# Attention over 31 pipelined steps: V's product in four visits, division on GpSimd, V's own copy of X

## The reference, cut to what matters

```
x1 = x + sum_h softmax(mask(q_h k_h^T / 8)) v_h W_o,h + b_o     (q, k, v from the layer-normed x)
out = x1 + FFN(layernorm(x1))                                   (sigmoids, router, 8 experts, top 2)
```

## Time and profile before

| | us |
|---|---|
| median of 3 runs (1163.03 to 1163.51) | 1163.17 |
| the profiled execution | 1161.71 |
| its span | 1160.0 |
| TensorE busy | 1039.1 (90%) |
| VectorE busy | 903.1 (78%) |
| ScalarE busy | 703.5 (61%) |
| GpSimd busy | 658.7 (57%) |

### The profile page before, as it was taken

How to read it: one execution, slowest core, us unless ns; L and a number is a source line. 1 busy time by engine, 2 the same in 40 slices (tenths; PEclk the granted TensorE clock), 3 DMA queues, 4 the chain that set the end, 5 groups by cost and what they waited for, 6 DMA issues and landing times.

```text
span 1160.0 us, 51334 instructions
## 1 busy us (share of the span) xinstructions
PE 1039.1 (90%) x19852; PEld 772.4 (67%) x19852; DVE 903.1 (78%) x2180; ACT 703.5 (61%) x1474; POOL 658.7 (57%) x658
## 2 busy tenths in 40 slices
PE   5689999999999999999999999999999848699984
PEld 3577777777777777777777777777777636354542
DVE  6878888888888888888888888888888863547573
ACT  4656666666666666666666666666666542577664
POOL 5766666666656666666666666665666202244644
PEclk9999999999999999999999999999999877899998
DMA  7677777777777776777777777777777740132422
GB/s 172 164 182 172 174 169 173 169 173 172 171 167 181 165 175 168 168 168 168 168 170 174 175 172 170 171 169 172 173 173 170 179 91 21 38 84 47 91 50 60
DMA packets 127279, 173.06 MB, mean 149 GB/s; under 512 B 46096, under 2 KB 57360, under 8 KB 127248
## 3 DMA queue, kind: packets, MB, share of 16 engines
q1 hardware_dynamic: 127248, 172.67, 64.3%
HBM read 117.67 MB, written 21.36 MB: 120 GB/s over the span
## 4 chain that ended last, share of the span: by engine, by line
PE 71%; DVE 13%; DMA 5%; issue 5%; ACT 3%; SPq 2%; POOL 1%; DVEq 0%; POOLq 0%; ACTq 0%
PE ZB L658 25%; PE SPS L641 12%; PE SPS L642 10%; PE ZB L626 8%; DVE PTZ L918 4%; PE ZB L631 4%; DMA XTB<-xt_scratch 4%; PE ZB L666 3%; DVE SSB L975 2%; SPq L416 2%; PE SPS L817 1%; PE SPS L791 1%; PE ZB L832 1%; PE ZB L826 1%; PE ZB L809 1%
## 5 line engine op out<-in xcount | busy, mean ns | idle before, releaser
L975 DVE CUSTOM_DVE_ANT_0 SSB<-SPS,MASK 128x640 f32<-128x640 f32 (+7 forms) x512 | 372.0, 745 | 124.6 <-PE SPS L642 111.1
L641 PE MATMUL SPS<-KHP,QS 128*128 (+2 forms) x768 | 326.2, 430 | 33.5 <-DVE NM L975 28.7
L658 PE MATMUL ZB<-PTZ,VR 32*64 32x256 f32 (+2 forms) x16384 | 322.7, 295 | 21.4 <-DVE PTZ L918 19.0
L1278 ACT ACTIVATE PRL<-SSB,NM 128x640 f32<-128x640 f32 (+3 forms) x256 | 253.3, 989 | 144.9 <-DVE NM L975 144.4
L658 PEld LDWEIGHTS ZB<-PTZ,VR 32*64 32x64 f32 x16384 | 271.5, 131 | 69.3 <-issue 53.9
L483 POOL TENSOR_TENSOR X<-X,OT 128x512 f32 (+1 forms) x64 | 81.9, 1279 | 342.3 <-ACT OT L1288 333.9
L642 PE MATMUL SPS<-KLP,QS 128*128 (+2 forms) x768 | 261.4, 348 | 0.0
L918 DVE STREAM_TRANSPOSE PTZ<-PRL 128x640 f32<-128x640 f32 (+3 forms) x256 | 258.6, 1030 | 0.0
L1278 ACT ACTIVATE PRS<-SSB,NM 128x128 f32<-128x128 f32 (+3 forms) x256 | 142.5, 559 | 154.4 <-DVE NM L975 154.4
L641 PEld LDWEIGHTS SPS<-KHP,QS 128*128 128x128 f32 x768 | 145.3, 189 | 110.9 <-issue 47.2
L466 POOL TENSOR_TENSOR QS<-RAW,QS 64x512 fp32r<-64x512 f32 x128 | 165.3, 1292 | 10.3
(11 more groups left out here) (167 smaller groups left out, 999.6 us busy)
## 6 DMA issues: line engine op xcount, KB each, us to landing
VR<-v_scratch SPq DMA_DIRECT2D x256, 256.0 KB, 5.6
KHP<-KHP SPq DMA_DIRECT2D x64, 256.0 KB, 3.2
KLP<-KLP SPq DMA_DIRECT2D x64, 256.0 KB, 3.9
v_scratch<-V SPq DMA_DIRECT2D x32, 512.0 KB, 7.7
RSB<-rcp_scratch SPq DMA_DIRECT2D x64, 256.0 KB, 4.0
XTB<-xt_scratch SPq DMA_DIRECT2D x62, 256.0 KB, 3.4
VR<-gate_scratch SPq DMA_DIRECT2D x16, 512.0 KB, 5.9
WQK<-in_W_q SPq DMA_DIRECT2D x33, 64.0 KB, 3.2
```

Of the source, the lines that this page charges most:

```text
L641: pe.matmul(SP_[n % 2][:, c0:c0 + wc], q, kh[:, c0:c0 + wc], start=True, stop=False)
L658: last = pe.matmul(ZB[h * DH:(h + 1) * DH, i, kt * TR:QT * TR], VR[rows, j, kt, h * DH:(h + 1) * DH], turned_block(h, kt, j, rows), start= ...
L975: v.tensor_tensor_reduce(out=SSB[n % 2][:, 0:w], in0=SP_[n % 2][:, 0:w], in1=MASK[:, S - w:S], scale=1.0, scalar=BIG, op0=ALU.add, op1=ALU ...
L1278: act.activation(exps_of(n), SSB[n % 2][:, 0:w], ACT.Exp, bias=NM[:, col:col + 1], scale=-1.0, accum_out=L[:, col:col + 1]).then_inc(exp_d ...
```

## The change

- **TensorE.** Units 5 and 6 are computed ahead of the product with V, whose blocks are now visited as 0 and 1; 2 and 3; 4 and 5; 6 and 7. At the step's end the order is unit 13, V, units 14 and 15, output projection (before: units 13 and 14, V, output projection, unit 15).
- **Division.** ScalarE copies the undivided product from ZB to the place in PTZ where the divided one stood (`act_z`, two copies), ahead of exponential 12. GpSimd divides there, in place (`divide`, two instructions of 128x512), ahead of its first `add_out`. VectorE's four instructions go. V's product waits for the first copy only.
- **ScalarE.** Exponential 15 moves from behind piece 0 of the next body to between the two output copies, which both move behind exponential 14.
- **VectorE.** Turn 13 moves ahead of mask 0, masks 5 and 6 ahead of turns 0 and 1, turns 2 and 3 behind masks 7 and 8, turn 8 ahead of mask 11, mask 15 ahead of turn 12.
- **V's X.** V reads a second copy of X transposed, XW, loaded once per step in one DMA of 512 KB (`stage_xv`). XTB is reloaded as soon as the four pieces of Q and K have read it. `spread_sums` waits in addition until GpSimd is past the last division, since that reads RSB.

```diff
         def stage_x(sp, it, c):
-            sp.wait_ge(v_filled, it * 2 + c - 1)
+            if isinstance(it, int) and it == 2:
+                sp.wait_ge(v_filled, 3 + c)
+            else:
+                sp.wait_ge(qk_filled, it * 4)
+                sp.nop(nofuse=True)
+            sp.dma_start(XTB[:, c * CH:(c + 1) * CH], xt_dram[:, part]).then_inc(x_staged[c], DMA)
+
+        def stage_xv(sp, it):
+            sp.wait_ge(v_filled, it * 2)
             sp.nop(nofuse=True)
-            sp.dma_start(XTB[:, c * CH:(c + 1) * CH], xt_dram[:, part]).then_inc(x_staged[c], DMA)
+            sp.dma_start(XW[:, :], xt_dram[:, bass.ds(((it // HP) % B) * S, S)]).then_inc(xv_staged, DMA)
...
+        def divide(gp, it, g):
+            gp.wait_ge(z_copied, it * 2 + 2)
+            gp.wait_ge(r_spread, it * (2 * DMA) + 2 * DMA)
+            gp.nop(nofuse=True)
+            z = ZN[g].rearrange("p (t i r) -> p i t r", i=P // TR, r=TR)
+            gp.tensor_tensor(z, z, RSB[:, g, :].rearrange("p (i t r) -> p i t r", t=TC, r=TR), ALU.mult).then_inc(zn_done, 1)
...
                 if not first:
+                    divide(gp, it - 1, 0)
+                    divide(gp, it - 1, 1)
                     add_out(gp, it - 1, 0)
...
-            values(0, 1)
             scores(5, 6)
...
-            values(2)
+            values(0, 1)
             scores(7, 8)
...
-            values(3)
+            values(2, 3)
...
-            scores(13, 14)
+            scores(13)
             v_of(0)
             v_of(1)
+            scores(14, 15)
             out_of(0)
             out_of(1)
-            scores(15)
...
+            turn_back(13)
             mask(0)
...
-            turn_back(13)
             turn_back(14)
...
-            turn(6, 7)
+            turn(6, 7, 8)
             stats(5)
             mask(11)
-            turn(8)
             mask(12)
...
-            for k in range(4):
-                zn(k)
             turn(9)
...
+            mask(15)
             turn(12)
-            mask(15)
...
+        def act_z(act, it, k):
+            banks = slice(2 - k * 2, 4 - k * 2)
+            act.wait_ge(pv_done, it * QT + QT)
+            act.activation(PTZ[:, QT * 9 * P:QT * 9 * P + 2 * CH].rearrange("p (q i r) -> p i q r", i=P // TR, r=TR)[:, banks],
+                           ZB[:, banks, 0:QT * TR].rearrange("p i (q r) -> p i q r", r=TR), ACT.Copy).then_inc(z_copied, 1)
...
-            exps_to(11, 13)
+            exps_to(11, 12)
+            if not first:
+                act_z(act, it - 1, 0)
+                act_z(act, it - 1, 1)
+            exps_to(12, 13)
             v_of(0)
...
             v_of(1)
-            out_of(0)
...
             exps_to(14, 15)
+            out_of(0)
+            exps_to(15, 16)
             out_of(1)
```

More of the change, by code:

```diff
@@ L214, in build_program @@
         x_staged = [sem(f"x_staged{c}") for c in range(2)]
+        xv_staged = sem("xv_staged")
         keys_spread = [sem(f"keys_spread{c}") for c in range(2)]
@@ L222, in build_program @@
         v_early = sem("v_early"); v_late = sem("v_late")
-        pv_done = sem("pv_done"); zn_done = sem("zn_done")
+        pv_done = sem("pv_done"); z_copied = sem("z_copied"); zn_done = sem("zn_done")
         bias_filled = sem("bias_filled"); bias_ready = sem("bias_ready")
@@ L331, in spread_sums @@
             sp.wait_ge(r_written, it * (2 * DMA) + 2 * DMA)
+            if isinstance(it, int) and it == STEPS - 1:
+                sp.wait_ge(zn_done, it * 2)
+            else:
+                sp.wait_ge(q_split, it * 4 + 8)
             for h in range(2):
@@ L368, in body @@
                 else:
+                    if not last:
+                        stage_xv(sp, it + 1)
                     spread_sums(sp, it - 1)
@@ L378, in body @@
                     spread(sp, it + 1, 1 - par, 1)
+                    if not first:
+                        stage_x(sp, it + 2, 0)
+                        stage_x(sp, it + 2, 1)
                 spread_v(sp, it, half, par, 0)
-                if not last:
+                if first:
                     stage_x(sp, it + 2, 0)
@@ L574, in _ @@
             norm_in(1, 1)
+            divide(gp, STEPS - 1, 0)
+            divide(gp, STEPS - 1, 1)
             add_out(gp, STEPS - 1, 0)
@@ L628, in pe_v @@
         def pe_v(pe, it, s, bank):
+            xt = XTB if isinstance(it, int) and it < 2 else XW
             for k in range(TC):
                 t = s * TC + k
-                last = pe.matmul(bank[:, k * P:(k + 1) * P], XTB[:, t * P:(t + 1) * P],
+                last = pe.matmul(bank[:, k * P:(k + 1) * P], xt[:, t * P:(t + 1) * P],
                                  WV[:, bass.ds((it % HP) * 2, 2), :].rearrange("p h e -> p (h e)"), start=True, stop=True)
@@ L663, in pe_out @@
         def pe_out(pe, it, g, bank):
-            pe.wait_ge(zn_done, it * 4 + 4)
+            pe.wait_ge(zn_done, it * 2 + g + 1)
             for i in range(TC):
@@ L710, in v_of @@
                 else:
-                    pe.wait_ge(zn_done, it * 4 - 2)
+                    pe.wait_ge(z_copied, it * 2 - 1)
+                    if s == 0:
+                        pe.wait_ge(xv_staged, it * DMA)
                 pe_v(pe, it + 1, s, ZB[:, 2 + s, :])
@@ L1036, in back @@
                     dve_reciprocal(v, it - 1, 1 - par)
-            def zn(k):
-                if not first:
-                    dve_zn(v, it - 1, k)
+            turn_back(13)
             mask(0)
@@ L1060, in dve_step @@
             stats(1)
-            if first:
-                mask(5)
+            mask(5)
+            mask(6)
             turn(0, 1)
-            if not first:
-                mask(5)
-            mask(6)
             stats(2)
-            turn(2, 3)
             stats(3)
@@ L1071, in dve_step @@
             mask(8)
+            turn(2, 3)
             turn(4, 5)
@@ L1210, in _ @@
             dve_low(v, 0, 0)
-            for k in range(4):
-                dve_zn(v, it, k)
             gates_1(v, 0)
@@ L1319, in act_step @@
                 qk(0)
-                act_exp(act, it - 1, 1 - par, UNITS - 1)
                 exps_to(0, 1)
@@ L1350, in act_step @@
             exps_to(14, 15)
+            out_of(0)
+            exps_to(15, 16)
             out_of(1)
-            if last:
-                act_exp(act, it, par, UNITS - 1)
         @block.scalar
@@ L1431, in _ @@
             turn_of(1)
+            act_z(act, STEPS - 1, 0)
+            act_z(act, STEPS - 1, 1)
             act_out(act, STEPS - 1, 0, Z)
```

8 lines of the change are left out of this document (removed).

## The result

| | us |
|---|---|
| before, median of 4 runs (1163.03 to 1171.34) | 1163.34 |
| after, median of 4 runs (1234.02 to 1240.31) | 1236.16 |
| ratio, with its 95% interval | 1.0622 (1.0588 to 1.0655) |
| profiled execution of after, span 1238.6 | 1240.31 |

The change makes the kernel 6.2% slower. The prediction had the direction and a place for it, but 1210 us, with a range up to 1224: the loss is 73 us where 47 were forecast. The profiled execution is the slowest of the four, 4 us above their median; sums over its trace explain 1240.31, not 1236.16.

A forecast was written before the change was run, and what follows sets the result against it. The prediction took the kernel as bound by TensorE with a thin cover at the seam of two bodies. 1161.71 profiled + 46.4 (29 steps) + 2.7 (tail) - 1.4 (body 31) = 1209.4, plus 1.5 to the median: 1210; range 1166 to 1224.

The forecast's parts named there:

- Points 4 and 5: At the seam: GpSimd's add starts at 514.28 (before 513.12); piece 2 waits for the second output copy, 516.28 instead of 515.39.
- Point 6: VectorE: turn 15 ends at 520.15, masks 3 and 4 behind it, so the 0.62 us wait becomes longer, on masks.
- Point 7: GpSimd's splits of Q end at 519.75, holding piece 3's bias copy and exponential 1; mask 3 starts at 521.08, not 520.63.
- Point 8: Behind mask 3, units 5 and 6: the product with V starts at 522.70 instead of 519.90, 2.80 us later.
- Point 9: Unit 9 starts at 530.33, 1.79 us later; a step takes 30.0 us against 28.40 on average, +46.4 us over 29.
- signs of being wrong: Prediction wrong if product with V starts within 6.5 us of piece 0, or piece 2 follows piece 1 without gap.
- The unseen costs: GpSimd's divisions 0 to +1.1 us per step, taken as 0; XW's reload nothing; behind the last step +2.7, body 31 -1.4.
- The port lock: GpSimd and VectorE share ports exclusively; could delay GpSimd's add some 1.2 us per step, 35 us in all; left out.
- the sum: Whole kernel: 1161.71 + 46.4 + 2.7 - 1.4 = 1209.4 us; median 1.5 above, 1210.9, stated as 1210.
- The open circle: Seam rival: second copy in time, piece 3 not waiting for the splits; step 28.56 us, 1169 us in all; chance 13%.
- The division as a gate: Rival: GpSimd's division over 2 us each makes the output's second half wait, 0.5 us per step, 1225 us; chance 3%.
- The faster case: Rival: VectorE's lead reaches mask 4, no seam stop; saves 0.62, 0.20, 0.6; step 26.8, 1118 us (half: 1140); chance 16%.

The follow-up runs named there:

- e5: The changed kernel with ScalarE's first output copy ahead of exponential 14 again and five filler matmuls between units 4 and 5: 1200.95 us, ratio 1.0336.
- e3: The changed kernel with five filler matmuls of 512 columns between units 4 and 5, their result overwritten: 1213.63 us, ratio 1.0448.
- e1: The changed kernel with ScalarE's first output copy put back ahead of exponential 14: 1232.9 us, ratio 1.0595.
- e10: The changed kernel with the filler matmuls, piece 2 waiting for the first output copy only and piece 3 for the second: 1238.59 us, ratio 1.0623.
- e4: The kernel before with V's own copy of X alone (XW, XTB reloaded early): 1157.97 us, ratio 0.9956.
- e7: V's own copy and GpSimd's division, with a new order of the loop's bodies meant to leave no engine waiting at the seam: 1116.78 us, ratio 0.9599.
- e8: The kernel before with own copy, GpSimd's division and units 5 and 6 ahead of the product in four visits: 1205.35 us, ratio 1.0363.
- e6: The kernel before with V's own copy and GpSimd's division with ScalarE's two copies, otherwise the old order: 1146.84 us, ratio 0.9852.
- e9: e8 with five filler matmuls between units 4 and 5, their result overwritten: 1171.9 us, ratio 1.0055.

## Why the prediction was right in direction and too small

It was right about the order and wrong about the clock. The starts that its points give, beside those on the trace of after, whose piece 0 starts at 526.81. In the trace of before, piece 0 starts at 513.26 in the same view, and the schedule starts it where the old body did, so the forecasts stand 13.55 us later here. The line of before, in that view:

```profile
513.26 1.02 PE L626 MATMUL ZB<-XTB,WQK 128*128 128x512 f32 x2
```

| point | forecast + 13.55 | measured |
|---|---|---|
| 4, GpSimd's add starts | 527.83 | 527.69 |
| 5, piece 2 starts | 529.83 | 529.71 |
| 6, turn 15 starts | 532.54 | 532.69 |
| 7, splits of Q end | 533.30 | 533.15 |
| 7, mask 3 starts | 534.63 | 534.52 |
| 8, product with V starts | 536.25 | 536.29 |
| 9, unit 9 starts | 543.88 | 543.67 |

**Points 4 and 5** hold within 0.14 us. The first output copy behind exponential 14 delays GpSimd's add; e5 against e3 gives that move a price of 0.5 us per step, and e1's full-clock steps 0.44.

**Point 6** is where the prediction chose, and it held: the wait for turns went (19.0 us to none), and the waits for masks grew (28.7 to 77.1). Turn 15 was 0.15 us later than laid out; it cost nothing, because point 7 comes later still.

**Point 7** was laid out as the link that decides. The chain goes through it, and e10 takes the other link away without a gain: without the wait before piece 2 the full-clock step is the same. That point 5's wait appears in the profile with 21.8 us says nothing of its price.

**Point 8.** From piece 0 to the product the order of time has 9.48 us now and had 6.64 before (513.26 to 519.90; the chain of the earlier trace rows dates piece 0 at 513.43), so +2.84 against +2.80.

**Point 9** and the step: 29.96 against 30.0. Unit 9 came 0.2 us sooner than laid out, so the agreement of the step to 0.04 is in part luck. Of the signs of being wrong neither came: the product with V starts 9.48 us behind piece 0, and piece 2 has its gap. Ahead of unit 5 about 2 us of idle time were forecast and 1.56 came. The second wait that was forecast, ahead of unit 6, is not among the idle times: unit 6 follows unit 5 at 535.62.

**The unseen costs.** The division took 1.29 us where 1.28 was taken and 0 to +1.1 on the path was the bound; TensorE waits for it only behind the last step, 3.1 us. XTB's wait was worth 0.18 per step (e4). Behind the last step 3.0 us were added and 1.3 forecast.

The port lock of the Trainium skill (SBUF — State Buffer, "SBUF: two separate sides"), weighed and left out, shows no sign here either: GpSimd's adds took 1.27 us on the mean and its divisions 1.29, and the add at 533.35 took 1.27 us although VectorE's turn 15 ran until 533.9.

**The step that failed** is the sum: it counts 29 steps at 30.0 us, and so takes every matmul to be as long as in the earlier trace rows. The loss by TensorE's clock is a term that it put at nothing, without a reason. "I lay the new order out on the old clock" is right for the instants, and was carried over to TensorE's speed. The schedule itself had over 2 us of idle time at the seam where the old one had its 0.6 for the turn and one short wait for a mask, and nothing in it asked what that does to the granted clock.

The runs show this in its place: the clock fell in 15 of 29 steps and in body 1. Against steps of 29.96 that is 1.53 us each, 23.0 us in all, and body 1 is 6.9 longer; e3, which holds the clock, gives 26 us of these back. Body 1's remaining 1.4 is near what the order costs any other step (1.56), and the sum left this body out. Together with the start (2.3) and the tail (1.7 more than forecast), less 1.2 for a step of 29.96 in place of 30.0 and 1.8 for the last, this is the whole 30.9 us between 1209.4 and the profiled 1240.31. With the clock held the same order takes 1213.6 us (e3), 4 from the forecast. The range failed with the sum: 1185 to 1224 allowed 0.3 us per step for errors of the schedule, and no rival was about the clock.

**The rivals.** The open circle (1169) did not occur: even with the copy first and the clock held, a step is 29.5. The division as a gate did not occur. The faster case (26.8 us per step, 1118) did not occur in this order. e7 takes 26.75 and 1116.8, but by another order of the lists, and the terms of the price don't close: 0.62 and 0.6 are more than the 1.07 between 6.47 and 5.4, and by the schedule's own durations the work there is 4.7 us (four pieces 3.44, units 0 to 4 1.27). So that the two figures are so close is in part luck; e7 shows that a step of that length can be had, not that this rival's mechanism gives it.

**What stays open.** Why the clock falls in some steps and not in others of the same kernel: in every second step of after, about two of three of e8, five of six of e1. In after the gap ahead of unit 5 is 1.55 to 1.57 us in most steps that keep the clock and 1.58 to 1.60 in most that lose it, but this difference of 0.03 belongs to the loop's two bodies and is in e3 too (0.41 and 0.44), and in e1 and e8 the gaps are alike in both kinds of step. Of the 2.16 us that the order loses per step at full clock, units 5 and 6 make 0.46 and the copy's place 0.44 to 0.5; the rest, the new places of exponential 15, of the masks and turns, and of units 14 and 15, was not taken apart. Nor was the start's 2.3.

## What to carry to other kernels

When units of work are moved ahead of a wait to fill it, look up where the work that *releases them* stands on its engine: here their masks stood behind the very turn that was to be waited out, so a wait of 0.6 us at the product became one of 1.4 ahead of unit 5 (e6 against e8). Before summing such a schedule, look at the idle time that it leaves on TensorE: where one gap grows to the 1.4 to 1.6 us that stood here in every kernel whose steps lost the clock, put a case with the lower clock beside the sum. And read the full-clock step and the clock's loss apart, in each experiment; otherwise a gain in order can vanish in the clock, as in e1.

## What the runs showed of the hardware

- In after the granted clock fell from 1.00 to 0.57, for some 4 us, right behind a seam with gaps of 0.78, 0.43 and 1.59 us. Each fall cost 1.4 to 1.5 us here, and over a run falls took 22.5 us (after against e3) and 33 us (e8 against e9).
- Of the 28 steps behind body 1, the last left out, the clock fell in 15 in after, 23 in e1, 19 in e8 and 11 in e10. All four kernels have a gap of 1.4 to 1.6 us ahead of unit 5; the smaller gaps before it differ (0.78 and 0.43; 0.59 and 0.43; 0.28; 0.43). In the same steps of the eight other kernels it fell in none; their gaps are at most 0.85 us, but for one of 1.09 in before.
- Whether it falls in a given step isn't decided by the size of the gap: in e1 and e8 steps with the same 1.38 us kept it and lost it. Why is open.
- Idle time filled with five matmuls of no use kept the clock when it left 0.44 us (e3), and not when 1.5 us stayed behind them (e10).
- A division in place on a permuted view, 128x512 on GpSimd, took 1.29 us, like a plain add of that size (1.27).
